# Turning the attention weights on VectorE in blocks of 32 by 32, with the column moves divided anew and some loads issued earlier, in a criss-cross attention kernel

## The reference

```python
q = einsum('oc,bchw->bohw', Wq, x) + bq        # 64 channels
k = einsum('oc,bchw->bohw', Wk, x) + bk        # 64 channels
v = einsum('oc,bchw->bohw', Wv, x) + bv        # 512 channels
energy_H = einsum('bchw,bcgw->bhwg', q, k) - 1e30 * eye    # along the column
energy_W = einsum('bchw,bchv->bhwv', q, k)                 # along the row
att = softmax(concatenate([energy_H, energy_W], -1), -1)
out = einsum('bcgw,bhwg->bchw', v, att_H) + einsum('bchv,bhwv->bchw', v, att_W)
return gamma * out + x
```

## Time and profile before

| | |
|---|---|
| time, median of 3 runs | 4050.99 us (4048.87 to 4056.91) |
| profiled execution: its time, its span from first to last instruction | 4051.03 us, 4049.3 us |
| TensorE busy, weight loads busy | 96%, 95% |
| VectorE, ScalarE, GpSimd busy | 60%, 41%, 15% |
| mean granted TensorE clock | 0.979 |
| moved by DMA | 874.33 MB, 216 GB/s |

### The profile page before, as it was taken

The page is one execution under the profiler, slowest core; times in us unless marked ns, Lnnn a source line. Parts: engine busy times, 40 slices in busy tenths (PEclk is TensorE's granted clock), DMA queues, the critical chain, the costliest instruction groups (busy, mean ns, idle before and its releaser), DMA issues.

```text
span 4049.3 us, 72640 instructions
## 1 busy us (share of the span) xinstructions
PE 3870.5 (96%) x28440; PEld 3839.0 (95%) x28440; DVE 2429.3 (60%) x5084; ACT 1667.5 (41%) x3658; POOL 624.2 (15%) x793
## 2 busy tenths in 40 slices
PE   5689999999999999999999999999999999999999
PEld 5679999999999999999999999999999999999999
DVE  4454677446773566745676467754667446783544
ACT  4452445424444244442444334542445424444111
POOL 0131003200042000310013100221003210031000
PEclk7799999999999999999999999999999999999999
DMA  4376775867758777687767777677775867759665
GB/s 138 104 200 203 256 251 185 233 212 240 243 180 229 224 245 230 195 222 232 244 219 209 214 242 241 213 218 211 249 242 188 234 209 250 240 180 238 199 201 172
DMA packets 256803, 874.33 MB, mean 216 GB/s; under 512 B 34256, under 2 KB 108496, under 8 KB 256464
## 3 DMA queue, kind: packets, MB, share of 16 engines
q1 hardware_dynamic: 256464, 869.67, 69.3%
HBM read 661.92 MB, written 207.62 MB: 215 GB/s over the span
## 4 chain that ended last, share of the span: by engine, by line
PE 90%; DMA 4%; DVE 4%; issue 1%; ACT 1%; POOL 0%; SPq 0%; DVEq 0%; ACTq 0%; POOLq 0%
PE bank L890 38%; PE bank L859 16%; PE bank L878 16%; PE bank L808 11%; PE bank L818 3%; PE bank L845 3%; PE bank L827 3%; DMA Pe<-e_scratch 2%; DMA XA<-in_x 1%; DMA out<-Y 1%; DVE Sx L590 1%; DVE E L609 1%; DVE mx L604 1%; DVE zs L618 0%; DVE Sy L595 0%
## 5 line engine op out<-in xcount | busy, mean ns | idle before, releaser
L890 PE MATMUL bank<-Sy,Wv_hi 128*128 128x384 f32 x6144 | 1595.1, 340 | 11.9 <-DVE Sy L595 11.9
L890 PEld LDWEIGHTS bank<-Sy,Wv_hi 128*128 128x128 f32 x6144 | 1087.9, 188 | 13.1 <-issue 13.1
L890 PE MATMUL bank<-Sy,Wv_lo 128*128 128x384 f32 x3072 | 1029.0, 335 | 0.0
L675 DVE SCALAR_TENSOR_TENSOR Y<-bank,bv_sb,Y 128x384 f32<-128x384 f32 x768 | 472.0, 615 | 872.2 <-PE bank L890 871.7
L878 PE MATMUL bank<-Pt,XT_r 128*128 128x96 f32 x6144 | 725.9, 275 | 15.6 <-DVE Y L666 9.4
L372 POOL TENSOR_TENSOR Pe<-Pe,F 96x384 f32<-96x384 f32 x384 | 319.3, 834 | 2701.8 <-DMA Pe<-e_scratch 2668.2
L878 PEld LDWEIGHTS bank<-Pt,XT_r 128*128 128x128 f32 x6144 | 705.6, 192 | 18.8 <-DVE Y L666 11.0
L496 ACT ACTIVATE Sy<-Y 128x768 fp32r<-128x768 f32 x384 | 302.8, 835 | 834.6 <-PE bank L890 799.8
L658 DVE COPY Y<-bank 128x96 f32<-128x96 f32 x1536 | 317.6, 321 | 499.3 <-PE bank L859 499.3
L890 PEld LDWEIGHTS bank<-Sy,Wv_lo 128*128 128x128 f32 x3072 | 576.8, 188 | 0.0
L808 PE MATMUL bank<-Sx,Wqk_hi 128*128 128x384 f32 x1536 | 425.0, 359 | 74.4 <-DVE Sx L590 74.4
(11 more groups left out here) (52 smaller groups left out, 3015.5 us busy)
## 6 DMA issues: line engine op xcount, KB each, us to landing
XA<-in_x SPq DMA_DIRECT2D x192, 768.0 KB, 5.4
Y<-in_x SPq DMA_DIRECT2D x192, 768.0 KB, 6.0
XT_r<-in_x_row SPq DMA_DIRECT2D x384, 384.0 KB, 5.4
out<-Y SPq DMA_DIRECT2D x192, 768.0 KB, 3.6
XT_r<-in_x_col SPq DMA_DIRECT2D x192, 384.0 KB, 4.8
XT_c<-in_x_col SPq DMA_DIRECT2D x192, 384.0 KB, 4.8
e_scratch<-E SPq DMA_DIRECT2D x384, 144.0 KB, 2.6
Pe<-e_scratch SPq DMA_DIRECT2D x384, 144.0 KB, 6.2
```

Source lines behind the costliest of these rows:

```text
L675: nc.vector.scalar_tensor_tensor(at, proj_ps[c % 2][:, 0:CP], bv_sb[:, c:c + 1], at, op0=ALU.add, op1=ALU.add).then_inc(out_made, 1)
L890: last = nc.tensor.matmul(proj_ps[c % 2][:, 0:CP], w[:, ct, at], Sy[:, lo, ct, :], start=(ct == 0 and k == 0), stop=(ct == CT - 1 and k == 2))
```

## The change

`turn` moves from TensorE to VectorE. It reads the scaled weights and writes Pt directly, in nine block transposes of 32 partitions by 4 times 32 elements. Bank 7, `copy_turned` and the semaphore `p_turned` go; a Pe buffer is now free when the turn is made (`pt_made`). Each turn waits for the scaled weights and for the last matmul that used the Pt buffer.

```diff
+            def turn(b, i):
+                dve.wait_ge(p_scaled, past(p_scaled, p_no(b, i)))
+                dve.wait_ge(o_summed, past(o_summed, o_no(b, (i - 2) * ROWS + ROWS - 1)))
+                to = Pt[:, i % 2, :].rearrange("p (r n) -> p r n", r=ROWS)
+                for h in range(0, N, BLOCK):
+                    for g in range(0, N, BLOCK):
+                        last = nc.vector.transpose(to[g:g + BLOCK, :, h:h + BLOCK],
+                                                   Pe[h:h + BLOCK, i % PRING, :, g:g + BLOCK])
+                last.then_inc(pt_made, 1)
```

In VectorE's program, column stage and row stage:

```diff
                 for g in range(CHUNKS):
+                    turn(b, g + 1)
                     move_column(b, g * ROWS)
-                    move_column(b, g * ROWS + 2)
...
             def row_stage(b, more):
-                dve.wait_ge(c_moved_act, past(c_moved_act, (b + 1) * (N // 2)))
+                turn(b, CHUNKS + 1)
+                dve.wait_ge(c_moved_act, past(c_moved_act, (b + 1) * (N - CHUNKS)))
...
                 add_row(b, 1, 3)
+                turn(b, CHUNKS + 2)
                 for n in range(CHUNKS):
...
                     if a_now:
                         sum_z(b + 1, a_now[0])
+                    if n + 3 < CHUNKS:
+                        turn(b, CHUNKS + n + 3)
                     finish(b, n, 2)
...
                     if turn_now:
                         factors_of_rows(b + 1)
+                        turn(b + 1, 0)
                     finish(b, n, 3)
```

ScalarE moves columns r = 1, 2 and 3 of each group. The queue SP:

```diff
             def column_stage(b):
-                for i in range(RRING, CRING):
+                load_xtc(b, RRING)
+                load_p(b, PRING)
+                for i in range(RRING + 1, CRING):
                     load_xtc(b, i)
-                load_xres(b, 0)
                 for g in range(CHUNKS):
-                    load_p(b, g + PRING)
+                    if g:
+                        load_p(b, g + PRING)
...
+                    if g == CHUNKS // 2:
+                        load_xres(b, 0)
...
-                    if more and n + 1 == A_FIRST:
+                    if more and n + 2 == A_FIRST:
                         load_xa(b + 1, 0)
                         load_xa(b + 1, 1)
```

More of the change, by code:

```diff
@@ L25 @@
 RBANKS = 3
+BLOCK = 32
 A_FIRST, A_LAST = 6, 17
@@ L109, in criss_cross_attention, with xa, sx @@
         oc_ps, or_ps, proj_ps = (*bank[0:3], bank[5]), bank[0:RBANKS], bank[3:5]
-        ec_ps, t_ps = bank[5:7], bank[7]
+        ec_ps = bank[5:7]
         st_ps, f_ps = bank[5], bank[6]
+        def xa(a, m):
+            return XA_first[:, m % 4 - 2, :, :] if a == 0 and m % 4 >= 2 else XA[:, m % 2, :, :]
+        def sx(a, m):
+            return Sx_first if a == 0 and m % 2 else Sx
         def qk_ps(a, m):
@@ L132, in criss_cross_attention @@
         xa_in = [sem(f"xa_in{j}") for j in range(2)]
+        xa_first_in = [sem(f"xa_first_in{j}") for j in range(4)]
         x_hi_made, x_lo_made, x_half_used = sem("x_hi_made"), sem("x_lo_made"), sem("x_half_used")
@@ L312, in prologue @@
                 sp.dma_start(bv_sb[:, :], bv).then_inc(small_in, 16)
-                load_xa(0, 1, before=False)
+                for m in range(1, 4):
+                    load_xa_first(m)
                 sp.dma_start(raw_v[:, :, :], wv_t.rearrange("(t p) n -> p t n", p=P)).then_inc(wv_in, 16)
                 for m in range(CHUNKS):
-                    if m + 2 < CHUNKS:
-                        load_xa(0, m + 2)
+                    if m + 4 < CHUNKS:
+                        load_xa_first(m + 4)
                     if m:
@@ L757, in prologue @@
                 low_x(0, 0)
+                for m in range(CHUNKS):
+                    if m + 1 < CHUNKS:
+                        low_x(0, m + 1)
+                    shift(0, m, before=False)
+                    if m:
+                        sum_z(0, m - 1)
+                sum_z(0, CHUNKS - 1)
                 dve.wait_ge(wv_in, 16)
@@ L766, in prologue @@
                 dve.wait_ge(gbv_made, 1)
-                for m in range(CHUNKS):
-                    if m + 1 < CHUNKS:
-                        low_x(0, m + 1)
-                    shift(0, m, before=False)
-                    if m:
-                        sum_z(0, m - 1)
-                sum_z(0, CHUNKS - 1)
                 for g in range(CHUNKS):
@@ L781, in prologue @@
                 factors_of_rows(0)
+                turn(0, 0)
             def whole(b):
@@ L807, in project_kq @@
                     for n, (w, lo) in enumerate(((Wqk_hi, 0), (Wqk_hi, 1), (Wqk_lo, 0))):
-                        last = nc.tensor.matmul(ps[:, 0:CP], w[:, ct, :], Sx[:, lo, ct, :],
+                        last = nc.tensor.matmul(ps[:, 0:CP], w[:, ct, :], sx(a, m)[:, lo, ct, :],
                                                 start=(ct == 0 and n == 0), stop=(ct == CT - 1 and n == 2))
@@ L839, in turn_factors @@
                 nc.tensor.transpose(f_ps[0:N, 0:N], st[0:N, 0, :], ident[:, :]).then_inc(f_turned, 1)
-            def turn(b, i):
-                pe.wait_ge(p_scaled, past(p_scaled, p_no(b, i)))
-                pe.wait_ge(pt_made, past(pt_made, p_no(b, i - 1)))
-                for r in range(ROWS):
-                    last = nc.tensor.transpose(t_ps[0:N, r * N:(r + 1) * N], Pe[:, i % PRING, r, :], ident[:, :])
-                last.then_inc(p_turned, 1)
             def attend_column(b, g, r):
@@ L894, in column_stage @@
             def column_stage(b):
-                turn(b, 0)
                 pe.wait_ge(r_added, past(r_added, b * N))
@@ L898, in column_stage @@
                 for g in range(CHUNKS):
-                    turn(b, g + 1)
                     for r in range(ROWS):
@@ L906, in row_stage @@
                 for n in range(2):
-                    turn(b, CHUNKS + n + 1)
                     for r in range(ROWS):
```

82 lines of the change are left out of this document (40 added, 42 removed).

## The result

The changed kernel takes 4086.31 us (median of 6 runs, 4073.03 to 4096.35), the kernel before 4052.64 us in the same comparison (6 runs, 4048.87 to 4056.91). The ratio is 1.008, 95% interval [1.006, 1.0101]: slower by 0.8%. The forecast was 4050 us, no change. The profiled execution took 4088.87 us, with a span of 4087.2 and a mean granted clock of 0.978.

The account below looks back on a forecast made before the run. The prediction took TensorE, busy 96% of the span, to bound the kernel. Gains in the column stages and losses in A and B iterations summed to -1 us against 4051.03: 4050 us, range 3900 to 4140.

Parts of the forecast that it names:

- columns, steady groups: Column stage, 192 groups: a loop over two groups takes 7.62 us, 3.81 a group instead of 3.91; -19 us.
- columns, start: turn 1 +7, weights 3 -50, pieces +5: Column stage's start: late first move and group 1 +7, no wait for weights 3 -50, pieces 4 and 5 behind it +5.
- columns, residual in group 12: Column stage: the 768 KB residual load ahead of weights 16 makes their turn 1.9 us late; +10 us over 8 batches.
- turn 26 at the row stage's start: Iteration 0: turn 26 stands ahead of the first `finish`, and TensorE's third projection waits 0.7 us; +6 us.
- plain iterations: 63 plain row iterations with a turn: 0.22 of the 0.34 us taken off TensorE is left; -14 us.
- iteration 5: Row iteration 5: earlier XA load ends 12 us of waits, but turn and `low_x` delay row 3 by 9; -3 us.
- A iterations: 84 row iterations (6 to 17 of a batch): the turn outlasts VectorE's gap by 0.54 us; +0.49 each, +41 us.
- B iterations: 21 row iterations with a turn (18 to 20 of a batch): VectorE needs 16.6 us instead of 15.7; +19 us.
- prologue: Prologue: chunks stay 7.05 us apart despite more buffers, only the start gains; -3 us.
- The price of a turn: VectorE's time T for nine transposes: 2.82 us, 0.313 each without overlap, with 1.8 and 3.2 as ends.
- both rivals with another price: Transposes overlap, T = 1.8, 3906 us (chance 0.20); or VectorE becomes the bound, T = 3.2, 4175 us (0.14).
- the loads do not help: Column stage's start: weights 3 late as before, behind the output store and piece 3; 4095 us, chance 0.05.

Follow-up runs that it names:

- experiment 7: The changed kernel with the turn's two loops over its nine blocks exchanged: 4087.59 us, ratio 1.0082.
- act_all: The changed kernel with all four column moves on ScalarE, none on VectorE: 4041.05 us, ratio 0.9971.
- late_turn: The changed kernel with each row iteration's turn at the end of VectorE's iteration instead of ahead of the third `finish`: 4062.39 us, ratio 1.0022.
- b_on_tensor: The changed kernel with the turns of iterations 18 to 20 back on TensorE in the first seven batches: 4044.46 us, ratio 0.9987.
- block_order: The changed kernel with the loops over g and h in the turn exchanged, so mostly the input's start partition changes: 4087.59 us, ratio 1.0082.
- res_last: The changed kernel with all column moves on ScalarE, turns late in iterations 6 to 20, and the residual loaded in the column stage's last group: 3971.69 us, ratio 0.9803.

## Why the prediction was wrong

Its sum of terms, beside the differences of the stages between the two profiled executions (span +37.9 us). Iterations of the last batch are counted as plain.

| term | predicted | measured |
|---|---|---|
| columns, steady groups | -19 | -1 |
| columns, start: turn 1 +7, weights 3 -50, pieces +5 | -38 | -28 |
| columns, residual in group 12 (groups 13 to 18) | +10 | +27 |
| turn 26 at the row stage's start | +6 | -1 |
| plain iterations | -14 | -12 |
| iteration 5 | -3 | -3 |
| A iterations | +41 | +19 |
| B iterations | +19 | +43 |
| prologue | -3 | -6 |
| sum | -1 | +38 |

The measured rows are rounded one by one.

**The price of a turn was right**, and with it both rivals with another price fell: 0.301 us long, 0.315 apart, T = 2.82. The number was the sum from the earlier trace rows, two instructions of ScalarE, only chose between three candidates; that it hit to 0.01 us is luck in part, and the reason for the missing overlap isn't shown (experiment 7). Plain iterations, iteration 5 and the prologue came out within 3 us of the steps, and the chunks kept their period. A steady plain iteration gained 0.32 us instead of 0.22, and iteration 0, with turn 26 ahead of it, takes 12.44 us beside 11.94 in the others; the table has both under plain iterations.

**First failed step: the loads, -50 + 5 + 10.** The wait for weights 3 did go ("No wait of 4 to 6 us for weights 3" came true). But the step priced the whole stall as one late transfer, and left 5 us over eight batches for what stands behind it. Pieces and weights share the queue: with weights 3 in time, weights 4 reach the scaling 7.9 us after their issue, and half of the stall stays (57.3 to 29.9 us in batches 1 to 7). The second half of the step, the residual chunk ahead of weights 16, was mis-sized too: the turn was to be 1.9 us late, and was 2.38; but the stage was to lose 1.3 us, and loses 3.8 in batch 1 and 27 over all, since 1.6 us come behind the wait, most of them at the lower clock (0.67 in group 16). Together the loads brought nothing where 35 us were forecast. The rival "the loads do not help" (4095 us, given 0.05) came near the time by its number and not by its reason: weights 3 were not late. How much of the 27 us gained at the start comes from the new order and how much from the residual chunk's leaving stays open.

**Second: the groups, -19, the loop's parts mis-sized.** The loop was the right one, and act_all shows that it binds. Its four parts were each a little short: from the group's first matmul to the turn 773.46 - 769.57 = 3.89 instead of 3.84, the turn and the step to the move 2.85 instead of 2.82, the move 0.91 instead of 0.83, the rest 0.15 instead of 0.13. That is 7.80 instead of 7.62, and with it the whole gain of 0.10 a group is gone. With a gain that small, the move's price had to be known to 0.1 us.

**Third: B iterations, +19, "VectorE needs 16.6 us in place of 15.7".** This took the busy sum for the length, as if VectorE's queue could run without a gap. In batch 1 VectorE is busy for 48.1 us of the stage, 16.0 an iteration and thus less than forecast, and an iteration takes 17.8 (+2.0, not +0.9). The turn stands ahead of the third `finish`, a `shift`, `low_y` and the first `add_row`, so TensorE waits for `add_row` (4.8 us in the stage) and its clock falls to 0.97, while VectorE still waits for projections and `round_y` and has gaps between its instructions, 5.2 us in all. The Trainium skill bears on a part of it (SBUF — State Buffer, section Who interferes with whom). It says that a VectorE instruction with two inputs in SBUF contends with a GpSimd instruction that reads SBUF. The trace agrees as far as it goes: in the iteration above `low_y` takes 1.44 us beside GpSimd's work, 0.96 in the kernel before, and GpSimd's copy beside it 1.57 instead of 0.88. By an estimate from these numbers, 0.5 of the 2.18 us by which row 3 is late would be that. No run separated it from the rest. late_turn and b_on_tensor settle the larger point: the turn in VectorE's queue is the cause (without it all 42 us are back), about a third of it by its place (6.1 to 4.2 us a batch over iterations 18 to 22). The rest stayed in both places that were tried; that it is due to the turn's length alone isn't shown.

**A iterations, +41, right mechanism, too large.** Measured +0.28 for a steady iteration instead of +0.49. The turn starts while `sum_z` is ending, and delays the third `finish` by 0.42 instead of 0.54 (538.73 - 534.75 = 3.98 behind the second, where it was 3.56). Another 0.09 has no row that names it. The last A iteration of a batch gained 0.32 instead. That a turn after the last `add_row` costs nothing there, and gains 0.16, was not seen: I kept the place that the change gave it and asked only what it delays.

The forecast was near no change because a gain of 47 that didn't come stood against a loss of 60. That loss came as large as forecast (61 us) only by luck: A was 22 us too high and B 24 too low.

## What to carry to other kernels

Work that leaves the bounding engine gains only if no loop through the engine that takes it over is as long; here the same turns lose 0.8% or, with the moves on ScalarE, the turns of the A iterations behind `add_row`, 21 turns left on TensorE and the residual chunk loaded at the column stage's end, gain 2.7%. In an engine that will be busy for 90% of a stage, follow the queue step by step: its busy sum gives a floor, and the waits and small gaps between its instructions, 5.2 us of 53.4 here, come on top. When a load is late in a stage whose DMA engines are busy for 0.9, price the load behind it too: here the changed loads left half of the stall, 768 KB moved to the stage's middle cost what had been gained, and moved out of the stage they gave 27 us.

## What the runs showed of the hardware

- 32x128 float32 block transposes on VectorE take 0.301 us and start 0.315 apart, whether mostly the output's start partition changes from one to the next (after) or mostly the input's (block_order).
- The column move of four copies took 0.90 us on VectorE between turns (median of 192), and 0.83 before (median of 384). Why isn't shown.
- `low_y` took 1.44 and 1.13 us in a B iteration with GpSimd active, 0.96 and 0.95 in the kernel before, and GpSimd's copy (L370) 1.57 us in place of 0.86 to 0.89 in the same stretch.
- The DMA engines moved 253 to 258 GB/s at a busy share of 1.00 to 1.04 (column stages of act_all and res_last), in loads of mostly 384 and 144 KB, and 236 at 0.88 (before).
- Behind a wait of 2.26 us TensorE's granted clock was 0.67 on average in a group of 5.24 us; two steady groups of 3.90 us had 1.00.
